# Last layer's first step of a graph network: TensorE fetches two of twelve tiles of source rows, GpSimd gathers ten, and four PSUM banks of the inner layers become two

## The reference, cut to what matters

```python
def _kernel_net(edge_attr, kW1, kb1, kW2, kb2, kW3, kb3):
    h = jax.nn.gelu(edge_attr @ kW1 + kb1)        # 6 -> 128
    h = jax.nn.gelu(h @ kW2 + kb2)                # 128 -> 128
    return h @ kW3 + kb3                          # 128 -> 16 x 16
w = _kernel_net(edge_attr, ...).reshape(-1, 16, 16)
for i in range(4):
    msg = jnp.einsum('ei,eio->eo', nodes[src], w)
    agg = jax.ops.segment_sum(msg, dst, num_segments=n) * inv_deg
    nodes = jax.nn.gelu(agg + nodes @ root_W[i] + root_b[i])
```

## Time and profile before

| | |
|---|---|
| median of three runs | 27560.11 us (27533.3 to 27577.4) |
| span of the profiled execution | 27543.6 us, mean granted TensorE clock 0.880 |
| busy: PE, DVE, ACT, POOL | 82%, 64%, 53%, 82% of the span |
| `kernel_net` pass | from 11893.88 (SyncE's first load) to 16979.9 us (last copy of VectorE), 5086 us |

### The profile page before, as it was taken

How to read it: one execution, slowest core, us unless ns; L and a number is a source line. 1 busy time by engine, 2 the same in 40 slices (tenths; PEclk the granted TensorE clock), 3 DMA queues, 4 the chain that set the end, 5 groups by cost and what they waited for, 6 DMA issues and landing times. The chain is left out here.

```text
span 27543.6 us, 413278 instructions
## 1 busy us (share of the span) xinstructions
PE 22500.5 (82%) x110422; PEld 12380.9 (45%) x110422; DVE 17653.1 (64%) x29340; ACT 14700.1 (53%) x24676; POOL 22669.1 (82%) x30933
## 2 busy tenths in 40 slices
PE   7888848888879999968888886888868888688886
PEld 3444435555556666634444443333333333343333
DVE  5555548888878888844444444666656666566665
ACT  6666601111117777733333333777757777577775
POOL 7888868888868888878888888888878888788887
PEclk9999979999989999977777777999989889799888
DMA  3111135555542222222322323555545555455554
GB/s 89 34 34 34 39 59 94 92 94 93 93 83 74 75 75 76 75 76 96 97 96 96 97 95 92 163 163 163 163 129 165 163 163 163 129 168 162 163 162 127
DMA packets 2192590, 2964.46 MB, mean 108 GB/s; under 512 B 778166, under 2 KB 1678244, under 8 KB 2190948
## 3 DMA queue, kind: packets, MB, share of 16 engines
q1 hardware_dynamic: 1340898, 2776.49, 30.8%
q0 software_dynamic: 782304, 157.92, 8.7%
q10 hardware_dynamic: 69282, 28.92, 0.4%
HBM read 2289.02 MB, written 672.64 MB: 108 GB/s over the span
## 5 line engine op out<-in xcount | busy, mean ns | idle before, releaser
L772 POOL DMA_INDIRECT got<-table,idx x14040 | 13761.8, 980 | 3764.0 <-issue 3473.8
L790 PE MATMUL in_place<-place_hot,tparts 128*128 128x512 fp8e4 x49950 | 12164.8, 405 | 2750.4 <-ACT place_hot L995 2462.5
L995 ACT ACTIVATE place_hot<-place_b,far_lanes 128x512 fp8e4<-128x512 f16 x17550 | 10959.8, 704 | 12.3 <-PE in_place L790 11.3
L790 PEld LDWEIGHTS in_place<-place_hot,tparts 128*128 128x128 bf16 x49950 | 5076.0, 103 | 9118.6 <-issue 4170.7
L775 POOL MEMSET rest<- 128x256 f32 x14040 | 4686.2, 334 | 8.3
L1599 POOL DMA_INDIRECT added<-rows,add_idx x2160 | 3599.9, 1667 | 719.3 <-issue 655.2
L1171 DVE TENSOR_TENSOR prod<-w_in,rows_p 128x2048 f32<-128x2048 f32 x810 | 1853.1, 2288 | 2837.4 <-issue 1522.9
L1216 DVE TENSOR_TENSOR prod<-wcopy,got 128x1024 f32<-128x1024 f32 x810 | 968.6, 1223 | 2603.3 <-DMA got<-table,idx 2324.8
L1642 PE MATMUL acc<-hot,spread 128*128 128x392 bf16 x12960 | 2533.4, 349 | 0.0
L859 PE MATMUL wmat<-k,h 128*128 128x256 f32 x6480 | 2045.2, 446 | 0.0
L1225 DVE TENSOR_REDUCE msg<-prod 128x64 f32<-128x1024 f32 x1620 | 1969.0, 1215 | 41.4
(11 more groups left out here) (250 smaller groups left out, 23056.3 us busy)
## 6 DMA issues: line engine op xcount, KB each, us to landing
w_in<-kept SPq DMA_DIRECT2D x2430, 512.0 KB
kept<-wcopy SPq DMA_DIRECT2D x810, 512.0 KB
got<-table,idx POOLq DMA_INDIRECT x14040
attr<-in_edge_attr SPq DMA_DIRECT2D x270, 768.0 KB
place_b<-place_row SPq DMA_DIRECT2D x1350, 128.0 KB
range_b<-range_row SPq DMA_DIRECT2D x1350, 128.0 KB
rows<-in_src_row SPq DMA_DIRECT2D x270, 512.0 KB
sums<-outb SPq DMA_DIRECT2D x1350, 96.0 KB
```

Of the source, the lines that this page charges most:

```text
L772: pool.indirect_dma_start(out=got[:, r, j * W:(j + 1) * W], out_offset=None, in_=table, in_offset=bass.IndirectOffsetOnAxis(ap=idx[:, r, j ...
L790: mm = pe.matmul(in_place[b][:, h, :], tparts[:, s, t, :], place_hot[:, b, t, h * XC:(h + 1) * XC], start=(t == 0 and s == 0), stop=(t == ...
L995: ins = act.activation(place_hot[:, b, t, :], place_b[:, b, :], ACT.Abs_reciprocal_sqrt, bias=SB["far_lanes"][:, t:t + 1], scale=HOT_SLOPE ...
```

## The change

In `kernel_net`, X becomes 2. GpSimd gathers ten tiles of a chunk, TensorE fetches the last two. The one-hots `place_hot` are made by VectorE here (`hot_lanes`, thirteen instructions of 128 x 256 a chunk, bfloat16 out), two chunks ahead. TensorE gets, after L3 of group 1, `in_row_sums` of this chunk and two thirds of `in_place_sums` of the next chunk (24 matmuls of 256 columns), and after L3 of group 2 the rest (13 matmuls). VectorE gets `fetch` ahead of the third product and `pick` for the next chunk at the end of a chunk. SyncE loads places and ranges and waits for `places_hot` and `picked_made` before it stores matrices. `h1p`, `h2p`, `in_place` and `in_row` have one bank each, so L1(m) now waits for `gelu1(m-1)`, and L2(m) for `gelu2(m-1)`. The start of the pass loads and splits the table, as in the other kinds.

```diff
-    X = {"weighted": 4, "relational": 4, "kernel_net": 0, "kernel_kept": 4}[kind]
+    X = {"weighted": 4, "relational": 4, "kernel_net": 2, "kernel_kept": 4}[kind]
-    AHEAD = 1 if kind == "relational" else 2
+    AHEAD = 1 if kind in ("relational", "kernel_net") else 2
+    LONE = kind == "kernel_net"
-            place_hot = sb("place_hot", [P, HALVES, KT, XE], F8)
+            place_hot = sb("place_hot", [P, HALVES, KT, XE], BF16 if LONE else F8)
-            h1p = [ps(f"h1p{k}", [P, GE]) for k in range(2)]
-            h2p = [ps(f"h2p{k}", [P, GE]) for k in range(2)]
+            h1p = ps("h1p", [P, GE])
+            h2p = ps("h2p", [P, GE])
...
-                    pe.wait_ge(S["h1_ready"], i * TURN_GROUPS + n + 1)
+                    pe.wait_ge(S["h1_ready"], i * TURN_GROUPS + n + 2)
...
-                    pe.wait_ge(S["h2_ready"], i * TURN_GROUPS + n + 1)
+                    pe.wait_ge(S["h2_ready"], i * TURN_GROUPS + n + 2)
...
                         layer3(i, n)
+                        if g == 1:
+                            in_row_sums(k, b)
+                        if g >= 1 and not (final and b == HALVES - 1):
+                            if g == 1:
+                                pe.wait_ge(S["places_hot"], k + 2)
+                            in_place_sums(1 - b, (0, 1) if g == 1 else (2,))
...
+                def hot_lanes(k, b, turn_no, first=False):
+                    dve.wait_ge(place_in[b], turn_no * 16 + 16)
+                    if not first:
+                        dve.wait_ge(S["in_place_made"], k - 1)
+                    for t in range(KT):
+                        ins = dve.tensor_scalar(place_hot[:, b, t, :], place_b[:, b, :], SB["lanes"][:, t:t + 1], HOT_IS, ALU.is_equal, ALU.mult)
+                    ins.then_inc(S["places_hot"], 1)
...
-                        if kind == "relational" and g == GROUPS - -(-X // G):
+                        if X and g == GROUPS - -(-X // G):
                             fetch(k, b, r)
                             dve.wait_ge(S["fetched"], k + 3)
                         product(g)
                         reduce(g - 1)
...
+                        if kind == "kernel_net" and g == 1 and (at is None or at + 2 < CHUNKS):
+                            hot_lanes(k + 2, b, i + 1)
...
+                if kind == "kernel_net":
+                    for b in range(HALVES):
+                        hot_lanes(b, b, 0, first=True)
                 if X:
                     split_table()
```

More of the change, by code:

```diff
@@ L604, in edge_pass @@
             range_b = sb("range_b", [P, HALVES, XE], F16)
-            place_hot = sb("place_hot", [P, HALVES, KT, XE], F8)
+            place_hot = sb("place_hot", [P, HALVES, KT, XE], BF16 if LONE else F8)
             picked = sb("picked", [P, XE])
-            in_place = [ps(f"in_place{k}", [P, XH * 512])[:, :].rearrange("p (h e) -> p h e", h=XH)[:, :, 0:XC] for k in range(HALVES)]
-            in_row = [ps(f"in_row{k}", [P, 512])[:, 0:X * FW] for k in range(HALVES)]
+            in_place = [ps(f"in_place{k}", [P, XH * 512])[:, :].rearrange("p (h e) -> p h e", h=XH)[:, :, 0:XC] for k in range(1 if LONE else HALVES)]
+            in_row = [ps(f"in_row{k}", [P, 512])[:, 0:X * FW] for k in range(1 if LONE else HALVES)]
+            if LONE:
+                in_place, in_row = in_place * HALVES, in_row * HALVES
             whole = SB["rows"][:, 0:KT * P].rearrange("p (t c) -> p t c", t=KT)
@@ L645, in edge_pass @@
                  "attr_used0", "attr_used1", "w_made", "w_used", "h1_made", "h1_ready", "h2_made", "h2_ready",
-                 "hot_made", "hot_used", "out_made", "stored0", "stored1", "dve_step", "run_cleared", "rested", "turn_open", "fetch_open",
+                 "hot_made", "hot_used", "out_made", "stored0", "stored1", "dve_step", "run_cleared", "rested", "turn_open", "load_open", "fetch_open",
                  "place_in0", "place_in1", "range_in0", "range_in1", "places_hot", "in_place_made", "picked_made", "in_row_made", "fetched",
-                 "added_clear", "kept0", "kept1", "kept2", "kept3", "mask_made", "scanned", "cleared", "w_copied", "bias_made", "rows_made", "whole_clear", "near_in", "far_in", "whole_step", "near_parts", "far_parts",
+                 "added_clear", "kept0", "kept1", "kept2", "kept3", "mask_made", "scanned", "cleared", "w_copied", "bias_made", "rows_made", "whole_clear", "near_in", "far_in", "whole_step", "bias_step", "near_parts", "far_parts",
                  "w_in0", "w_in1", "w_in2", "w_in3", "w_in4", "w_in5", "w_in6", "w_in7"]
@@ L679, in load @@
                             sp.wait_ge(attr_used[b], i)
+                        if kind == "kernel_net":
+                            sp.sem_inc(S["load_open"], 1)
                     if kind == "relational":
@@ L801, in in_row_sums @@
                     else:
-                        pe.wait_ge(S["fetched"], k + 1)
+                        pe.wait_ge(S["fetched"], k + (2 if LONE else 1))
                     pe.wait_ge(S["picked_made"], k + 2)
@@ L893, in layer1 @@
                         pe.wait_ge(attr_in[b], (i + 1) * 16)
-                    pe.wait_ge(S["h1_ready"], i * TURN_GROUPS + n + 1)
-                    mm = pe.matmul(h1p[n % 2][:, :], SB["k1"][:, :], attr[:, b, g * GE:(g + 1) * GE], start=True, stop=True)
+                    pe.wait_ge(S["h1_ready"], i * TURN_GROUPS + n + 2)
+                    mm = pe.matmul(h1p[:, :], SB["k1"][:, :], attr[:, b, g * GE:(g + 1) * GE], start=True, stop=True)
                     mm.then_inc(S["h1_made"], 1)
@@ L900, in layer2 @@
                     pe.wait_ge(S["h1_ready"], i * TURN_GROUPS + n + 3)
-                    pe.wait_ge(S["h2_ready"], i * TURN_GROUPS + n + 1)
-                    pe.matmul(h2p[n % 2][:, :], SB["k2"][:, :], h1[:, n % 2, :], start=True, stop=True).then_inc(S["h2_made"], 1)
+                    pe.wait_ge(S["h2_ready"], i * TURN_GROUPS + n + 2)
+                    pe.matmul(h2p[:, :], SB["k2"][:, :], h1[:, n % 2, :], start=True, stop=True).then_inc(S["h2_made"], 1)
                 def layer3(i, n):
@@ L906, in layer3, with net_turn @@
                     matrices(i * TURN_GROUPS + n, n % 2, h2[:, n % 2, :], [SB["k3"][:, :]])
-                pe.wait_ge(S["bias_made"], 1)
-                last = TURN_GROUPS
-                with pe.Fori(0, TURNS) as i:
+                def net_turn(i, final):
+                    last = TURN_GROUPS
                     layer1(i, 0)
@@ L914, in _ @@
                     for n in range(last):
+                        b, g = divmod(n, GROUPS)
+                        k = i * HALVES + b
                         if n + 2 < last:
@@ L919, in _, with load_whole @@
                         layer3(i, n)
+                        if g == 1:
[4 more added lines that the diff above has]
+                            in_place_sums(1 - b, (0, 1) if g == 1 else (2,))
+                pe.wait_ge(S["bias_made"], 1)
+                with pe.Fori(0, TURNS - 1) as i:
+                    net_turn(i, False)
+                net_turn(TURNS - 1, True)
             @block.scalar
             def _(act):
+                def load_whole():
+                    for t in range(1, NEAR, 2):
+                        act.dma_start(whole[:, t, :].rearrange("r (o f) -> r o f", o=OWNERS), table_v[t * P:(t + 1) * P, :, :]).then_inc(S["near_in"], 16)
+                    for t in range(NEAR + 1, KT - 1, 2):
+                        act.dma_start(whole[:, t, :].rearrange("r (o f) -> r o f", o=OWNERS), table_v[t * P:(t + 1) * P, :, :]).then_inc(S["far_in"], 16)
+                load_whole()
                 if kind == "kernel_net":
@@ L927, in gelu1 @@
                         act.wait_ge(S["h2_made"], i * TURN_GROUPS + n + 1)
-                        act.activation(h1[:, n % 2, :], h1p[n % 2][:, :], ACT.Gelu_apprx_tanh, bias=SB["b1"][:, 0:1]).then_inc(S["h1_ready"], 1)
+                        act.activation(h1[:, n % 2, :], h1p[:, :], ACT.Gelu_apprx_tanh, bias=SB["b1"][:, 0:1]).then_inc(S["h1_ready"], 1)
                     def gelu2(i, n):
@@ L933, in gelu2 @@
                         act.wait_ge(w_made, i * TURN_GROUPS + n + 1)
-                        act.activation(h2[:, n % 2, :], h2p[n % 2][:, :], ACT.Gelu_apprx_tanh, bias=SB["b2"][:, 0:1]).then_inc(S["h2_ready"], 1)
+                        act.activation(h2[:, n % 2, :], h2p[:, :], ACT.Gelu_apprx_tanh, bias=SB["b2"][:, 0:1]).then_inc(S["h2_ready"], 1)
                     def copy_out(i, n, first):
@@ L1015, in chunk @@
                         rows_over(k + 1, 1 - b, (r + 1) % RING, q + (r + 1) // RING, at == 0)
[L1017 to L1024, removed]
                 if kind == "weighted":
@@ L1055, in bias_as_rows @@
                 def bias_as_rows():
-                    c = Chain(dve, S["whole_step"])
+                    c = Chain(dve, S["bias_step"])
                     c.step(dve.memset(bias_rows[:, :, :], 0.0))
```

## The result

The changed kernel took 27779.45 us (median of four runs, 27777.83 to 27787.38) against 27553.15 us before (the three runs named above and a fourth): a ratio of 1.0083, 95% interval 1.0069 to 1.0098. It is slower by 226 us; forecast were 27766 us, slower with a chance of 0.71. The profiled execution spans 27785.6 us, 242 more than the one before, and the pass that was changed takes 5324 us (SyncE's first load at 11891.17 to the last copy at 17215.36) instead of 5086: 238 of the 242.

What follows compares the result with a forecast made beforehand. GpSimd was taken to bound the kernel before, TensorE after: 135 turns of 38.95 us, +3 at the end, -5077, give +184; +22 at the start gives +206, so 27766 us by the median; range 27460 to 28040.

Steps and rivals of the forecast that it cites:

- GpSimd bounds the kernel before, TensorE the one after: kernel_net pass: GpSimd sets 37.6 us a turn before; after, it needs 31.2 and TensorE 35.2 at full clock.
- TensorE's sum at the full clock: TensorE's turn in kernel_net: 25.3 before, plus in_place 8.1, in_row 0.9 and single-bank idle 0.95, making 35.2 us.
- The single banks: L1(1) at the turn's start waits for a gelu: 0.95 us idle a turn, no cost at other L1.
- The clock: TensorE at each turn's start: one low stretch of 7.5 us, costing 3.75 us, so the turn is 38.95 us.
- the first L3 ends the low stretch: TensorE's turn start: the L3 begun at 14039.39 ended the low stretch, and comes at the same place after.
- Rival A: L1(0) to L2(1) of each turn: the clock does not fall, turn 35.2 us, 27260 us; chance 0.13.
- VectorE's cover: VectorE's pick chain, about 7 us, hides behind 8.6 us of TensorE work, leaving 1.1 us of cover.
- rival C: More stalls in the turn: low stretch 10.2 us, one-hots at 0.72 us each; middle about 28150 us; chance 0.14.
- The start: Start of the pass: table split and chunk 0 fetched first, first L1 at about 31 us, 22 us later.
- What GpSimd waits for: GpSimd in the changed kernel: its idle would be ended by VectorE's got_used; no size given.

Runs made afterwards that it cites:

- a better clock: Kernel before with L1's weights and data padded by zeros from 6 to 128 rows, nothing else: 27589.17 us, ratio 1.0015.
- the order that holds the clock without the idle: Changed kernel with the next turn's L1(0), L1(1), L2(0) moved among and behind the in_place matmuls at the turn's end: 27126.15 us, ratio to before 0.9845.

## Why the prediction was right

The sign, the size and the mechanism held. The change of the time was +206 us by the forecast and +226 by the medians; in the profiled execution the pass grew by 238, of which the turn's 0.21 us too little (28 us in 135 turns) and the start's 3 us are what the forecast lacked. Step by step:

- **GpSimd bounds the kernel before, TensorE the one after.** Shown from both sides: seven more memsets a chunk changed nothing after, 48 fewer matmuls a turn made it faster, and a better clock gave nothing before.
- **TensorE's sum at the full clock**, 35.2 us, was 34.9. in_place cost 2.62 us for 24 (14035.51 to 14038.13 in the same trace), 0.109 each as taken, and 0.09 more where an L1 follows (2.71, 14019.54 to 14022.25). in_row was 0.36 us a chunk (14019.18 to 14019.54) where I had 0.45.
- **The single banks.** One idle of 0.78 us a turn, L1(1) 1.89 us after L1(0), 1.9 forecast; none within the turn. Alone they cost nothing in the kernel before.
- **The clock.** One low stretch a turn, from 2 to 4 us after L1(0). Its length was mis-sized: 8.6 us on average, taken was 7.5, so the price 4.3 instead of 3.75 us. I had cut the longer kind, 10.2 us, to 8.2 for the idle it held before; the 10.2 came back in full in 62 turns with no idle within it. The turn came to 39.16 against 38.95: by luck, this error and that of the sum at the full clock go opposite ways. That the first L3 ends the low stretch was argued from one turn. It ended 3.4 us after that L3's start there, 4.1 and 2.5 in the two turns above, and no run isolates what ended it.
- **Rival A** (the clock holds) did not come true in this order, and is worth what it was priced at in another: forecast 27260, with the idle still in it; the order that holds the clock without the idle took 27126, and 0.95 us of idle a turn are 128 of the 134 us between. The sentence of the Trainium skill that went with it ("TensorE: Matmul & The Clock Gate", HAM oscillation: no long idle gaps between bursts) is not enough here by the measurement: the clock fell in the kernel before at 14035.94, with TensorE busy without a gap since 14010.81, and held with 0.78 us of idle once L1 had 128 rows.
- **VectorE's cover.** The thirteen one-hots took 3.06 us (0.24 each, start to start) where I had 5.2; and the pick was never waited for. Already 5.2 left a cover by the forecast's own sum; with 3.06 rival C had less behind it than its 0.14. Here 0.24 is lower than both of my bounds (0.37 and 0.72), which were recorded durations, not steps from one start to the next.

```profile
14038.80 3.06 DVE L1124 TENSOR_SCALAR place_hot<-place_b,lanes 128x256 bf16<-128x256 f16 x13
```

- **The start** was 33.7 us to the first L1 (11891.17 to 11924.89), forecast 31; before it was 8.8. So +25 instead of +22.
- **What GpSimd waits for** I named wrongly: not `got_used`, but the index copy, which VectorE makes at a chunk's start.

The range of 27460 to 28040 was wider on the upper side than needed, as the one-hots cost a third of what rival C had them cost (3.06 us against 13 x 0.72 = 9.4).

## What to carry to other kernels

Before moving work onto an engine with busy time to spare, add up that engine's own steps from start to start over one period: here TensorE's 14% of idle time was less than the work that came, so the bound moved, and a low clock that had been free came to cost 4.3 us a turn, more than the whole loss of 1.7. Look at what stands in the places where the clock falls, not at idle time alone: matmuls with few rows of weights side by side were such a place here, and spreading them between dense ones, or padding them with zero rows, gave 650 to 770 us. Then the same move that lost 0.8% gains 2.2%.

## What the runs showed of the hardware that I had not expected

- Float32 matmuls with weights of 6 rows, beside the same matmuls padded to 128 rows: the granted clock at a turn's start went from 0.63 (14002 to 14012 us, changed kernel) to 1.00 (14028 to 14038 us, padded), with the same columns, order and idle. Padding cost TensorE nothing, its steps got shorter; in the kernel before it came with 39 us more, by longer gathers, the cause of which is open.
- An L1 with weights of 6 rows between matmuls with weights of 96 or 128 rows cost 0.25 us more than the same L1 padded (1.5 us for six in a turn): L1 to L2 took 1.05 us and 0.86 when both had 128 rows, the L2 behind it 0.96 and 0.86.
- Two kinds of turns, 38.4 and 40.0 us, in one steady loop of equal work: the low stretch was 6.8 or 10.2 us long, so the clock's contribution differs from turn to turn by half of 3.4 us. The later in the turn it began, the shorter it was: 10.2 us at 2.2 to 3.0 us after L1(0), 6.8 at 3.0 to 3.9, and with fewer matmuls 3.4 at 4.9 to 5.5.
- All gathers of GpSimd that took over 1.3 us (221 with a mean of 1.59 us in the kernel before, 230 with 1.69 in its padded form) overlapped a `product` of VectorE; the others took 0.97 us.
